# Expert stage of a language-model block: x turned by DMA instead of by TensorE, and the up product with the weights as the loaded operand

## What is computed

```
x_flat = layernorm(h).reshape(4096, 256)
topk_logits, topk_idx = top_k(x_flat @ router, 2)          # 8 experts, each token goes to 2
topk_weights = softmax(topk_logits)
x_sort  = x_flat[tokens sorted by expert]                  # 8192 rows
w13_out = ragged_dot(x_sort, w13)                          # 256 -> 1024, the expert's own weights
gate, up = split(w13_out, 2)                               # 512 and 512
hidden  = silu(gate) * up
out_dispatch = ragged_dot(hidden, w2)                      # 512 -> 256
out[token] += out_dispatch * weight_of_the_row             # scatter with addition
```

## Time and profile before

| | us |
|---|---|
| median of 3 runs (990.41 to 992.03) | 990.95 |
| the profiled execution, its whole time | 983.11 |
| its span in the trace | 981.4 |
| first up product to last down product | 655.5 to 972 |
| TensorE busy with matmuls | 809.6 (82%) |
| VectorE, ScalarE, GpSimd busy | 500.8, 590.8, 373.7 |

### The profile page before, as it was taken

One profiled execution on the slowest core, in us unless ns is written; L12 is line 12 of the kernel. 1 busy time (PEld: TensorE's weight loads), 2 busy tenths in 40 slices (PEclk: granted clock), 3 DMA queues, 4 the chain that ended last, 5 costly groups with the idle time before them and its releaser, 6 DMA issues. The chain is left out here.

```text
span 981.4 us, 18229 instructions
## 1 busy us (share of the span) xinstructions
PE 809.6 (82%) x5861; PEld 359.0 (37%) x5862; DVE 500.8 (51%) x1513; ACT 590.8 (60%) x591; POOL 373.7 (38%) x312
## 2 busy tenths in 40 slices
PE   4053989898899889999988996039999999999996
PEld 2052322222222222222222222016666666666664
DVE  5076034646455565564654556825545445455453
ACT  0031698898999999999998995113333333233332
POOL 6782200220222202222022215434555555555653
PEclk9995799999999999999999998559999999999998
DMA  1000101041101111101111014412333333333332
GB/s 24 2 1 20 44 2 33 11 34 44 44 25 30 34 44 44 44 12 33 45 44 35 20 34 87 125 37 48 56 58 57 59 54 58 59 56 53 58 48 28
DMA packets 33532, 40.32 MB, mean 41 GB/s; under 512 B 7199, under 2 KB 29361, under 8 KB 33474
## 3 DMA queue, kind: packets, MB, share of 16 engines
q0 software_dynamic: 16256, 17.55, 11.9%
q1 hardware_dynamic: 17218, 22.04, 8.7%
HBM read 22.79 MB, written 17.56 MB: 41 GB/s over the span
## 5 line engine op out<-in xcount | busy, mean ns | idle before, releaser
L886 ACT ACTIVATE shared<-PS 128x1536 f32<-128x1536 f32 x342 | 467.1, 1474 | 41.1 <-PE PS L690 39.7
L700 PE MATMUL PS<-shared,va 128*32 128x512 f32 x2048 | 277.3, 614 | 5.1 <-DVE acc_s L1126 4.8
L844 POOL DMA_INDIRECT slots<-pair_no,pos_i x64 | 63.4, 991 | 385.2 <-DVE pos_i L1013 348.0
L1253 PE MATMUL PS<-w_p,xsT 128*128 x828 | 191.2, 381 | 0.4 <-issue 0.4
L690 PE MATMUL PS<-qf,ak 32*128 32x512 bf16 x1024 | 131.3, 390 | 43.7 <-ACT shared L886 38.7
L1311 ACT ACTIVATE act_s<-PS 128x512 f32<-128x512 f32 x69 | 41.3, 598 | 153.4 <-PE PS L1253 153.4
L1216 POOL DMA_INDIRECT out<-y_s,idx_tok x68 | 108.3, 1592 | 54.8 <-issue 48.0
L1253 PEld LDWEIGHTS PS<-w_p,xsT 128*128 128x128 f16 x828 | 81.3, 98 | 85.1 <-issue 3.0
L1204 POOL DMA_INDIRECT xs<-xrows,idx_tok x70 | 73.2, 1046 | 95.7 <-DVE weight L1350 84.9
L690 PEld LDWEIGHTS PS<-qf,ak 32*128 32x128 bf16 x1024 | 31.6, 91 | 208.9 <-ACT shared L886 157.2
L1270 PE MATMUL PS<-shared,hidT 128*128 x828 | 101.7, 273 | 0.3 <-DVE hidT L1369 0.3
(11 more groups left out here) (273 smaller groups left out, 765.0 us busy)
## 6 DMA issues: line engine op xcount, KB each, us to landing
w_raw<-w SPq DMA_DIRECT2D x24, 512.0 KB, 4.4
xrows<-rows SPq DMA_DIRECT2D x16, 258.0 KB, 3.5
out<-h1s SPq DMA_DIRECT2D x16, 256.0 KB
xs<-xrows,idx_tok POOLq DMA_INDIRECT x70, 2.8
out<-y_s,idx_tok POOLq DMA_INDIRECT x68, 3.8
slots<-pair_no,pos_i POOLq DMA_INDIRECT x64, 6.5
cw<-coeff,xi POOLq DMA_INDIRECT x32, 2.3
wvT_s<-wvT SPq DMA_DIRECT2D x1, 256.0 KB, 2.9
```

The lines of the kernel that those rows point to most:

```text
L700: last = pe.matmul(PS[32 * slot:32 * slot + 32, ACC, :], g.va[:, KT * (grp // HG) + kt, c, :], prob[:, (4 * quad + slot) % (RING * WIDE), ...
L844: pool.indirect_dma_start(g.slots, bass.IndirectOffsetOnAxis(pos_i[:, grp % 2, 2 * k + kk:2 * k + kk + 1].bitcast(U32), 0), g.pair_no[:, t ...
L886: act.activation(prob[:, at:at + n, :].rearrange("p n q -> p (n q)"), PS[:, buf:buf + n, :].rearrange("p c q -> p (c q)"), ACT.Exp).then_i ...
L1253: last = pe.matmul(PS[:, up_bank(k) + half, :], xsT[:, k, 2 * a + c, :], g.w13_p[:, w, c, ds(e, 1), FF * half:FF * half + FF].rearrange("p ...
```

## The change

`experts_phase` is rewritten around four x buffers (`XBUF = 4`), and the loops run 17 times over four tiles. What changes per tile:

- x is turned by one DMA transpose issued by SyncE (128 rows × 512 fp16), not by four TensorE transposes and a ScalarE copy.
- In the up product the operands trade places: a 128×128 piece of `w13_p` is loaded, and 128 columns of `xsT` stream. The output comes out with the inner dimension on the partitions: 8 pieces of 128 columns, each 6 terms, 48 matmuls of 128 columns.
- `turn_hidden` goes (the product is already turned); VectorE reads the split's input from SBUF and not from PSUM.
- The row's weight is applied by ScalarE at the copy of the result (`scale=weight`), and no longer in `hidden`.
- GpSimd gathers four tiles ahead, and passes on the landed scatters itself, before each scatter.

```diff
-        with eng.Fori(0, USUAL // 2) as i:
+        with eng.Fori(0, USUAL // XBUF) as i:
...
+            def turn_x(k, arrived):
+                sp.wait_ge(xs_in[k], arrived)
+                sp.sem_inc(x_landed, 1)
+                sp.dma_start_transpose(xsT[:, k], xs[:, k, 0:4 * P]).then_inc(xT_in[k], 16)
...
             def scatter(m, apart):
+                if m >= 2:
+                    pool.wait_ge(y_out[m % 2], 16 * (m // 2))
+                    pool.sem_inc(y_free, 1)
...
+                    pool.wait_ge(weighed, j - XBUF + 1)
+                    pool.wait_ge(up_mm, j - XBUF + 1)
...
-            def up(k, e, copied, free):
-                pe.wait_ge(x_copied, copied)
+            def up(k, e, arrived, free):
+                pe.wait_ge(xT_in[k], arrived)
                 pe.wait_ge(hid_ready, free)
-                for half in range(2):
-                    terms = [(c, a, w) for c in range(2) for a, w in ((0, 0), (0, 1), (1, 0))]
+                for m in range(2 * FF // P):
+                    place = PS[:, up_bank(k) + m // 4, P * (m % 4):P * (m % 4) + P]
+                    terms = [(c, a, w) for c in range(2) for a, w in ((0, 0), (1, 0), (0, 1))]
                     for n, (c, a, w) in enumerate(terms):
-                        last = pe.matmul(PS[:, up_bank(k) + half, :], xsT[:, k, 2 * a + c, :],
-                                         g.w13_p[:, w, c, ds(e, 1), FF * half:FF * half + FF].rearrange("p e f -> p (e f)"),
-                                         start=n == 0, stop=n == len(terms) - 1)
+                        last = pe.matmul(place, g.w13_p[:, w, c, ds(e, 1), P * m:P * m + P].rearrange("p e f -> p (e f)"),
+                                         xsT[:, k, 2 * a + c, :], start=n == 0, stop=n == len(terms) - 1)
                 last.then_inc(up_mm, 1)
...
             def body(i):
-                for k in range(2):
-                    j = i * 2 + k
-                    up(1 - k, expert(j + 2), j + 2, j + FREE)
-                    turn_x(k, i * 16 + 32, j + 2)
-                    turn_hidden(k, j + 1 + FREE, j + FREE)
-                    down(1 - k, expert(j), j + FREE, j - 1 + FREE)
+                for k in range(XBUF):
+                    j = i * XBUF + k
+                    up((k + 1) % XBUF, expert(j + 2), i * 16 + 16 * ((k + 1) // XBUF + 1), j + FREE)
+                    down((k + 1) % 2, expert(j), j + FREE, j - 1 + FREE)
...
-                act.copy(y_s[:, k, :], PS[:, YB[k], 0:D]).then_inc(y_copied, 1)
+                act.activation(y_s[:, k, :], PS[:, YB[k % 2], 0:D], ACT.Copy, scale=weight[:, k:k + 1]).then_inc(y_copied, 1)
...
-                dve.scalar_tensor_tensor(hid[:, k, :], act_s[:, k, :], weight[:, k:k + 1], PS[:, up_bank(k) + 1, :],
-                                         ALU.mult, ALU.mult).then_inc(hid_ready, 1)
+                dve.tensor_tensor(hid[:, k, :], act_s[:, k, :], PS[:, up_bank(k) + 1, :], ALU.mult).then_inc(hid_ready, 1)
+                dve.wait_ge(y_mm, used)
+                dve.wait_ge(hid_ready, n + 1 + FREE)
+                dve.tensor_copy(hidT[:, k, 0:4].rearrange("p c q -> p (c q)"), hid[:, k, :]).then_inc(hid_step, 1)
```

More of the change, by code:

```diff
@@ L66 @@
 FREE = 2
+XBUF = 4
 WIDE, BUFS, RING = 3, 2, 5
@@ L1157, in experts_phase @@
     PS = g.PS
-    xs_w, xsT = tmp("xs", [P, 2, XW], I32), tmp("xsT", [P, 2, 4, P], F16)
+    xs_w, xsT = tmp("xs", [P, XBUF, XW], I32), tmp("xsT", [P, XBUF, 4, P], F16)
     xs = xs_w[:].bitcast(F16)
@@ L1161, in experts_phase @@
     hidT = tmp("hidT", [P, 2, 8, P], BF16)
[L1162 to L1165, removed]
+    y_s, weight = tmp("y_s", [P, XBUF, D]), tmp("weight", [P, XBUF])
+    xs_in, xT_in = [sem(f"xs_in{k}") for k in range(XBUF)], [sem(f"xT_in{k}") for k in range(XBUF)]
+    y_out = [sem("y_out0"), sem("y_out1")]
+    zeroed, up_mm, x_landed = sem("zeroed"), sem("up_mm"), sem("x_landed")
+    silu_done, hid_ready = sem("silu_done"), sem("hid_ready")
     hidT_ready, y_mm, y_copied, y_free = sem("hidT_ready"), sem("y_mm"), sem("y_copied"), sem("y_free")
     hid_step, weighed = sem("hid_step"), sem("weighed")
-    XB, HTB, YB = 0, 5, (6, 7)
+    YB = (6, 7)
     def up_bank(k):
-        return 1 + 2 * k
+        return 1 + 2 * (k % 2)
     def steps(eng, body, end):
         more = eng.value_load(g.more[0:1, 0:1], min_val=0, max_val=1)
-        with eng.Fori(0, USUAL // 2) as i:
+        with eng.Fori(0, USUAL // XBUF) as i:
             body(i)
         with eng.If(more > 0):
-            with eng.Fori(USUAL // 2, ETILES // 2) as i:
+            with eng.Fori(USUAL // XBUF, ETILES // XBUF) as i:
                 body(i)
@@ L1301, in _ @@
         def _(act):
-            def copy_x(k, turned, used):
-                act.wait_ge(x_turned, turned)
-                if used is not None:
-                    act.wait_ge(up_mm, used)
-                act.copy(xsT[:, k].rearrange("p c q -> p (c q)"), PS[:, XB, :].bitcast(F16)[:, 0:4 * P]).then_inc(x_copied, 1)
             def silu(k, up_done, free):
@@ L1353, in _ @@
             dve.memset(xs_w[:].bitcast(F32), 0.0).then_inc(zeroed, 1)
+            dve.memset(weight[:], 0.0).then_inc(zeroed, 1)
             dve.memset(hidT[:], 0.0).then_inc(zeroed, 1)
@@ L1356, in _ @@
             dve.sem_inc(hidT_ready, FREE)
-            weigh(0, 0, 1, None)
-            weigh(1, 1, 2, None)
+            dve.wait_ge(zeroed, 3)
+            weigh(0, 0, 16, None)
+            weigh(1, 1, 16, None)
             hidden(0, 0, FREE)
             def body(i):
-                for k in range(2):
-                    j = i * 2 + k
-                    weigh(k, j + 2, j + 3, j + 1 + FREE)
-                    dve.wait_ge(hid_turned, j + 1 + FREE)
-                    dve.wait_ge(y_mm, j + FREE)
-                    dve.tensor_copy(hidT[:, k, 0:4].rearrange("p c q -> p (c q)"), PS[:, HTB, :]).then_inc(hid_step, 1)
-                    dve.wait_ge(hid_step, j + 1)
-                    dve.tensor_tensor(hidT[:, k, 4:8].rearrange("p c q -> p (c q)"), PS[:, HTB, :],
-                                      hidT[:, k, 0:4].rearrange("p c q -> p (c q)"), ALU.subtract).then_inc(hidT_ready, 1)
-                    hidden(1 - k, j + 1, j + FREE)
+                for k in range(XBUF):
+                    j = i * XBUF + k
+                    weigh((k + 2) % XBUF, j + 2, i * 16 + 16 * ((k + 2) // XBUF + 1), j + FREE)
+                    hidden((k + 1) % 2, j + 1, j + 1 + FREE)
             def end(tiles):
```

84 lines of the change are left out of this document (34 added, 50 removed).

## The result

The changed kernel takes 1159.5 us (median of 4 runs, 1156.8 to 1162.5), the kernel before beside it 991.25 us: a ratio of 1.170, with an interval of 1.168 to 1.173. On another chip, beside the later experiments, the same pair gave 1154.1 and 988.1 us, a ratio of 1.168 (1.166 to 1.170). The forecast was 1153 us, in a range of 1128 to 1215. Of all executions recorded one, of the control further down, took 4048 us at a low granted clock; it counts in no ratio.

The account below looks back on a forecast made before the run. The prediction took TensorE's sequencer as the changed kernel's bound: 6.95 us a tile against 4.56, times 68, adds 162 us to 983.1, 1145 us profiled. With 7.8 us for the median, that made 1153 us, range 1128 to 1215.

Parts of the forecast that it names:

- The array is not the bound afterwards: Expert stage: TensorE's array would need 4.0 us a tile, less than its sequencer's 6.95.
- The address instruction, 0.125 us: Up product: each weight address costs TensorE's sequencer 0.125 us; 32 a tile in place of 8 make 4.0 us.
- Two reads, 1.5 us: Expert loop: reading the expert's number twice a tile costs TensorE's sequencer 1.5 us.
- The tile, 6.95 us: Expert stage: the sequencer's addresses, reads, waits and loop end sum to 6.95 us a tile, against 4.56 before.
- 68 tiles, +162 us: Expert stage: 2.39 us more a tile, times 68, adds 162 us.
- VectorE, ScalarE, GpSimd and the transposes at nothing: Expert stage: these engines' work and the DMA transposes, taken as 2.5 us a tile, stay hidden under 6.95 us.
- Start within 2 us: Start of the expert stage: extra gathers, larger memset and first transposes change the time by ±2 us.
- "The end is the same chain of scatters.": End of the expert stage: the same scatters follow as before, with no time added.
- The rival of the reloaded code: Expert loop: TensorE's code is fetched again on 17 returns, 25 to 75 us more, 1178 to 1228 us; 10 in 100.
- The array as the bound: Expert stage: shorter address spacing leaves the array's 4.0 us a tile as the bound, 953 us; 7 in 100.
- The clock: Expert stage: with the array busy 57%, its clock falls to half, 7.7 us a tile, 1203 us; 11 in 100.
- The transposes: Expert stage: x's DMA transpose is the bound, 1361 us at 10 us a tile, 2041 at 20; 9 in 100.

Follow-up runs that it names:

- the control further down: The kernel before, with its up product always reading expert 0's weights: 979.8 us beside 980.4 for the kernel before.
- the kernel without addresses: The changed kernel with both products always on expert 0's weights and no expert number read on TensorE: 953.0 us beside 988.1 for the kernel before.
- the sixteen that were taken out: The changed kernel with expert 0's weights for the up product's low bf16 halves only, leaving 16 address instructions: 1013.3 us beside 980.4 for the kernel before.
- the experiment: The changed kernel with six expert reads on TensorE in place of eight for each four tiles: 1136.5 us beside 990.0 for the kernel before.
- the run with the fixed up product: The changed kernel with the up product always reading expert 0's weights, expert number still read, down product unchanged: 998.2 us beside 980.4 for the kernel before.
- without the far path: The changed kernel without TensorE's untaken code for more than the usual number of tiles: 1150.8 us beside 1154.1 for the changed kernel.
- the one with copied weights: The changed kernel with VectorE first copying the tile's up weights into one of two fixed buffers: 972.4 us beside 988.1 for the kernel before; again, 975.8 beside 992.5.

## Why the prediction was right, step by step

- **The array is not the bound afterwards.** Right: it would run a tile in 3.99 us (predicted 4.0), as the kernel without addresses shows.
- **The address instruction, 0.125 us.** Right, and causally so: 0.125 us for each of the sixteen that were taken out. That the pace was read while the array ran at half clock is what made the sum safe.
- **Two reads, 1.5 us.** A little high: 0.67 us each by the experiment, 1.35 for both.
- **The tile, 6.95 us.** Measured 6.94, so the other small terms (waits, registers, the down product's addresses) were together a little low, by about 0.15 us. That the sum came out within 0.01 us is in part luck.
- **68 tiles, +162 us.** The middle is +162.4.
- **VectorE, ScalarE, GpSimd and the transposes at nothing.** Right; none of them is waited for, even at 3.99 us a tile. For the transposes the prediction took 2.5 us of the DMA engines' time a tile, from 512 packets of 79 ns. There are 541 packets a tile (31184 of SyncE's queue from 700 to 1100 us, in 57.65 tiles), and they take 9.5% of the DMA engines' time in that stretch, 0.66 us a tile, a quarter of the estimate: the count was right and the price was not. From issue to landing one tile's transpose takes 2.5 us. By the Trainium skill's 1309 ns for one 128×128 piece (VectorE: DVE Perf Modes, "The three transpose paths") four in turn would be an estimated 5.2 us; the trace does not agree, with 2.5 us for all four. Either was hidden.
- **Start within 2 us.** It is +1.4 us: the first up product waits for gather and transpose.
- **"The end is the same chain of scatters."** This step was wrong, by 5.2 us. The sum had no term for leaving the loop. The rival of the reloaded code had looked at the right mechanism in the wrong place: it charged 17 returns and not the one jump over the untaken path. Together with the start it is as much as the 6.5 us by which the median is above the forecast.
- **The rivals.** The array as the bound: no, 32 addresses keep 0.125 us each. The clock: it stayed at 1.00 with the array busy for 40.6 of 50 us. The prediction compared unlike shares: its 57% came from the array's bare 4.0 us, and the rows of before that it was held against count a matmul's whole record, here 225 ns for one matmul, of which 48 start within 4.0 us. The transposes: no. The 81 ns for a 128-column matmul of the Trainium skill (TensorE: Matmul & The Clock Gate, "Back-to-back issue gap"): the stream without addresses ran at 56 ns, so the row of the kernel before was the better source.

What the prediction did not see was that removing the addresses alone would not bring the array's bound back: the run with the fixed up product was forecast at the array's 4.0 us and took 4.69. The sum of a sequencer's work and the sum of the array's are two bounds only as long as the sequencer may run ahead; here it was through 1.15 us before the end of the up product.

## What to carry to other kernels

Count an engine's instruction stream as a resource of its own: before a wide matmul is cut into narrow ones whose addresses come from a register, multiply the new number of such instructions by their spacing in the trace (here 0.125 us), add the reads of registers (0.67 us), and compare with what the array needs. Busy shares don't show this party. If it is the bound, a copy of the indexed operand to a fixed place by an engine with time to spare can be much cheaper than the addressing. And look at the exit of a loop too: with a long untaken path between the loop and the code behind it, TensorE stood idle for 4.5 us, once.

## What the runs showed of the hardware that was not expected

- A register read of the expert's number, "TENSOR_LOAD", usually lasts 302 ns, but 680 ns where it ran beside the down product's matmuls in the kernel with the fixed up product. What lengthens it is open; in the changed kernel, where the array waits for the sequencer, all 58 reads from 700 to 900 us took 297 to 312 ns.
- With no address instructions between them, the sequencer is through with 48 load and matmul pairs when 17 of them are yet to start (1.15 us to the end of the last), the same in 50 tiles of the kernel with the fixed up product; everything else that it has to do waits for that.
- The jump over an untaken loop of 335 to 680 instructions of TensorE took 3.3 to 4.2 us in each of eleven profiled executions; the jump over the some 190 of the kernel before took 0.21 us, and 0.33 us in its control.
- A tile's time is nearly the same on every chip (4.567 us for the kernel before, with and without the fixed expert, 6.938 for the changed kernel in three executions, one of them without the far path; 4.189 and 4.209 for the one with copied weights), while the stages ahead of it took from 645.2 to 656.9 us. For a change within the loop the tile is the sharper measure.
- ScalarE copies 2048 bf16 columns in 1.90 us, VectorE in 0.71 us.
